# Second graph attention of a two-layer network: weighted sums of a head pair in two goes of 12 and 10 key tiles, earlier reciprocals, a bf16 mask

## What is computed

```python
qkv = x @ Wqkv + bqkv                                  # x: [2708, 256], 4 heads of 64
scores = einsum('hnd,hmd->hnm', qh, kh) * SCALE
scores = scores + graph_bias * adj_matrix
scores = where(attn_mask == 0, -1e9, scores)           # adj_matrix = attn_mask = adj
attn = softmax(scores, axis=-1)
out = einsum('hnm,hmd->hnd', attn, vh)
return out @ Wout + bout
```

## Time and profile before

| what | us |
|---|---|
| median of 3 runs (2942.5 to 2944.53) | 2943.89 |
| the profiled execution, own time | 2962.46 |
| its span, first to last instruction | 2960.5 |
| PE busy | 2559.8 (86%) |
| DVE busy | 2115.6 (71%) |
| ACT busy | 1793.5 (61%) |
| POOL busy | 1485.8 (50%) |

### The profile page before, as it was taken

The page is one execution under the profiler, slowest core; times in us unless marked ns, Lnnn a source line. Parts: engine busy times, 40 slices in busy tenths (PEclk is TensorE's granted clock), DMA queues, the critical chain, the costliest instruction groups (busy, mean ns, idle before and its releaser), DMA issues. The chain is left out here.

```text
span 2960.5 us, 62129 instructions
## 1 busy us (share of the span) xinstructions
PE 2559.8 (86%) x20638; PEld 2083.9 (70%) x20725; DVE 2115.6 (71%) x4364; ACT 1793.5 (61%) x3207; POOL 1485.8 (50%) x1752
## 2 busy tenths in 40 slices
PE   6698888888871599636899999999959999999999
PEld 5466666666661599416767777777748888888888
DVE  5799999999963244256587787787766777777776
ACT  1688888888840133114466666666646777777775
POOL 5755666665523311363122122122138888888886
PEclk9899999999985799757999999999989999999999
DMA  5011111111134222211011111111000000000001
GB/s 197 19 39 52 42 37 37 37 37 37 38 129 145 73 71 71 73 39 50 6 39 42 54 37 40 54 37 40 35 7 0 0 0 0 0 0 0 0 0 38
DMA packets 53520, 122.55 MB, mean 41 GB/s; under 512 B 7402, under 2 KB 38734, under 8 KB 47822
## 3 DMA queue, kind: packets, MB, share of 16 engines
q1 hardware_dynamic: 46350, 102.28, 10.0%
q0 software_dynamic: 7104, 19.41, 2.0%
HBM read 97.39 MB, written 24.27 MB: 41 GB/s over the span
## 5 line engine op out<-in xcount | busy, mean ns | idle before, releaser
L1974 PE MATMUL f_pm<-f_wl,f_yt 128*128 128x256 f32 x2640 | 625.7, 380 | 0.0
L1974 PEld LDWEIGHTS f_pm<-f_wl,f_yt 128*128 128x128 f32 x2640 | 477.2, 191 | 51.6
L515 POOL TENSOR_SCALAR a_off<-ADJ 128x677 bf16<-128x677 f32 x88 | 284.4, 3254 | 271.8 <-DMA ADJ<-in_adj 260.1
L1022 POOL TENSOR_TENSOR ADJ<-ADJ,a_off 128x2708 f32<-128x2708 f32 x22 | 131.3, 5969 | 537.4 <-DVE ADJ L1101 537.4
L116 POOL TENSOR_SCALAR f_yy<-f_th,f_rs 128x255 f32<-128x255 f32 x660 | 367.7, 575 | 21.8 <-POOL f_rs L111 21.8
L1824 DVE SCALAR_TENSOR_TENSOR f_gg<-f_th,f_pm 128x512 f32<-128x512 f32 x319 | 218.9, 686 | 167.8 <-ACT f_th L1918 166.7
L587 DVE SCALAR_TENSOR_TENSOR a_lg<-a_fo,F,a_low 128x1024 f32<-128x1024 f32 (+1 forms) x264 | 296.9, 1152 | 37.0 <-ACT a_low L536 23.5
L1918 ACT ACTIVATE f_th<-f_pm 128x512 f32<-128x512 f32 x319 | 190.6, 597 | 200.1 <-PE f_pm L1974 200.1
L1081 DVE CUSTOM_DVE_ANT_0 a_sc<-a_qk,ADJ 128x1024 f32<-128x1024 f32 (+1 forms) x264 | 288.1, 1092 | 30.7 <-PE a_qk L1179 30.7
L536 ACT ACTIVATE a_low<-a_fo,F2S 128x1024 f32<-128x1024 f32 (+1 forms) x264 | 259.0, 1018 | 78.7 <-PE a_fo L664 77.6
L1045 ACT ACTIVATE a_sc<-a_sc,a_mx 128x1024 f32<-128x1024 f32 (+1 forms) x264 | 277.7, 1052 | 42.3 <-DVE a_mx L1086 42.3
(11 more groups left out here) (256 smaller groups left out, 4986.9 us busy)
## 6 DMA issues: line engine op xcount, KB each, us to landing
ADJ<-in_adj SPq DMA_DIRECT2D x44, 1354.0 KB, 5.9
W<-in_L_ffn_w SPq DMA_DIRECT2D x32, 512.0 KB, 10.0
XD<-p_zeros SPq DMA_DIRECT2D x1, 7680.0 KB
m_rows<-XD SPq DMA_DIRECT2D x60, 128.0 KB, 2.0
YD<-m_y POOLq DMA_DIRECT2D x60, 128.0 KB, 2.0
out<-X SPq DMA_DIRECT2D x21, 128.0 KB
X<-in_x SPq DMA_DIRECT2D x3, 768.0 KB, 9.6
p_wqkv<-in_L_gnn_Wqkv SPq DMA_DIRECT2D x1, 768.0 KB, 4.4
```

Of the source, the lines that this page charges most:

```text
L515: pool.tensor_scalar(off[:, b, cols], adj[:, b, cols], 0.0, -HUGE, ALU.is_equal, ALU.mult).then_inc(off_done[b], 1)
L1974: mm = pe.matmul(out, yt[:, g, r, k, :], wl[:, k, :], start=(k == 0), stop=(k == KD - 1))
```

## The change

The weights of a pair get one buffer for all 22 key tiles. `weighted` runs twice per pair: tiles 0 to 11 (48 records of the trace) at the end of the pair's own chunk 2, tiles 12 to 21 (40 records) at the end of chunk 0 of the next pair. Chunk 1 has none. The reciprocals move on VectorE from chunk 1, behind `project`, to chunk 0, behind `heads`. The mask `off` becomes bf16 and its value -2^30.

```diff
-MASKED = -1e9
+MASKED = -2.0 ** 30
...
+HALF = 12
...
-        off = ph.sb("off", [P, N])
+        off = ph.sb("off", [P, N], BF16)
...
-        wt = ph.sb("wt", [P, 2, 2, CT, P])
+        wt = ph.sb("wt", [P, 2, NT, P])
...
-            copy(wt[:, (hp * NC + c) % 2, s, j - c * CT:end - c * CT, :],
+            copy(wt[:, s, j:end, :],
...
-                    if c == 0 and pair_before(i, b, hp):
-                        heads(*pair_before(i, b, hp))
+                    if c == 0:
+                        if pair_before(i, b, hp):
+                            heads(*pair_before(i, b, hp))
+                        reciprocals(i, b, hp)
                     if c == 1:
...
-                        reciprocals(i, b, hp)
...
-            def weighted(i, b, hp, c):
+            def weighted(i, b, hp, half):
 
-                if c == 0 and pair_before(i, b, hp):
+                if half == 0 and pair_before(i, b, hp):
                     pe.wait_ge(heads_out, pairs(*pair_before(i, b, hp)))
-                for g, (j0, end) in enumerate(chunk_groups(c)):
-                    for s in range(2):
-                        group = ("turn", hp, s, c, g)
-                        pe.wait_ge(copied[bank(group)], uses(i, b, group))
-                    for j in range(j0, end):
+                first, end = ((0, HALF), (HALF, NT))[half]
+                for c in range(NC):
+                    for g, (j0, j1) in enumerate(chunk_groups(c)):
+                        if max(first, j0) >= min(end, j1):
+                            continue
                         for s in range(2):
-                            mm = pe.matmul(po[s * HD:(s + 1) * HD, 0:P], V[:, j, 2 * hp + s, 0:HD],
-                                           wt[:, (hp * NC + c) % 2, s, j - c * CT, :],
-                                           start=(j == 0), stop=(j == NT - 1))
-                if c == NC - 1:
+                            group = ("turn", hp, s, c, g)
+                            pe.wait_ge(copied[bank(group)], uses(i, b, group))
+                        for j in range(max(first, j0), min(end, j1)):
+                            for s in range(2):
+                                mm = pe.matmul(po[s * HD:(s + 1) * HD, 0:P], V[:, j, 2 * hp + s, 0:HD],
+                                               wt[:, s, j, :], start=(j == 0), stop=(j == NT - 1))
+                if half:
                     mm.then_inc(heads_in, 1)
...
-                    if c:
-                        weighted(i, b, hp, c - 1)
-                    elif pair_before(i, b, hp):
-                        weighted(*pair_before(i, b, hp), NC - 1)
+                    if c == NC - 1:
+                        weighted(i, b, hp, 0)
+                    elif c == 0 and pair_before(i, b, hp):
+                        weighted(*pair_before(i, b, hp), 1)
...
-            weighted(NPAIR - 1, 1, HPAIR - 1, NC - 1)
+            weighted(NPAIR - 1, 1, HPAIR - 1, 1)
```

## The result

The changed kernel takes 3033.39 us, the median of six runs (3030.64 to 3039.96). The kernel before takes 2943.89 on the same chip, the median of five runs (2942.50 to 2945.22); a sixth run took 11528.47 us and is left out. The ratio is 1.0307, with a 95% interval of 1.0296 to 1.0318: 89.5 us slower. Forecast were 3053 us, and 3008 to 3096 as the range.

What follows compares the result with a forecast made beforehand. The second attention was taken as bound by VectorE's chain behind each anchor, then by TensorE's own work. Uncovered records 71.8, GpSimd 2.5 and clock falls 35 summed to +109 us on 2943.9: 3053 us, range 3008 to 3096.

Steps and rivals of the forecast that it cites:

- The chain behind the anchor: From TensorE's end of chunk 0's weighted sums, VectorE's work sets 7.86 or 6.13 us; freeing TensorE there gains 0.
- 32 records of 0.055 us, uncovered: Records moved to chunk 2 and next chunk 0, where TensorE never waits: 1.75 us in 41 pairs, +71.8 us.
- The clock: In the second attention, 41 new TensorE waits lower its granted clock, 1.7 us per fall: +35 us, between 0 and 70.
- I take half: Half of the 41 new TensorE waits are followed by a clock fall: 20.5 x 1.7 = +35 us.
- GpSimd: Mask addition with bf16 goes from 5969 ns to 8.4 us, hidden except once at the stage's start: +2.5 us.
- VectorE's bf16 write: Making the mask in bf16 stays at 1.56 us: 0; rival of halved rate +28 us, 3081, chance 0.04.
- the reciprocals: Moved on VectorE to chunk 0 behind `heads`: 0, at most 0.53 us per pair either way.
- The dropped go: One go of weighted sums fewer per pair on TensorE: 0.23 us beside its records, 0.3 taken as the most.
- the rival: TensorE alone bounds the second attention; a dropped go gives 0.3 us in 43 pairs: 13 us less, 2931, chance 0.06.

Runs made afterwards that it cites:

- e1: The changed kernel with the weighted sums back in the old three goes of 8, 8 and 6 tiles: 2944.92 us.
- e2: The changed kernel, with TensorE multiplying the first 8 tiles once more at the end of chunk 1, result thrown away: 3021.94 us.
- e5: The changed kernel with VectorE's mask and adjacency scaling moved from chunks 0 and 1 to the end of chunk 2 of pair hp = 1: 2965.79 us.
- e6: The changed kernel with VectorE taking project ahead of chunk 1's second score instead of behind it: 2992.57 us.
- e3: The changed kernel with the reciprocals back in chunk 1, behind project: 3036.57 us.
- e4: The kernel before with only the bf16 mask and its new value: 2941.33 us, ratio 0.9993.
- e9: The kernel before, three goes kept, with mask and scaling moved to chunk 2 and project ahead of chunk 1's second score: 2936.15 us.
- e8: The changed kernel with its go of 12 tiles at the end of chunk 1, 10 at the end of the next chunk 0: 2931.05 us.
- e10: e8 with goes of 8 tiles at the end of chunk 1 and 14 at the end of the next chunk 0: 2943.77 us.
- e11: e8 with VectorE's mask and scaling moved to the end of chunk 2 and project ahead of chunk 1's second score: 2975.03 us.
- e7: The changed kernel with VectorE's mask and scaling at the end of chunk 2 and project ahead of chunk 1's second score: 2932.06 us.
- e12: e11 with the reciprocals at the end of chunk 1: 2951.00 us.

## Why the prediction was right

**The chain behind the anchor, right.** Predicted were 7.86 and 6.13 us, unchanged; measured 7.91 and 6.07. Predicted were 20 waits ahead of `shares` and 21 ahead of chunk 2's turn, and about 1 us in the last block. There are 20 for `shares` and 21 for L1128, the last of them 1.21 us; the first block waits 2.07 us for the small copy that stands in `project`'s place there. e1 and e2 show from two sides that they, and not TensorE's work, set the stretch, and e5 and e6 that either is VectorE's own.

**32 records of 0.055 us, uncovered, right.** 41 x 1.75 = 71.8 us. The stage grew by 89.4, less 18.8 of clock: 70.6. Anchors were predicted 17.4 and 17.9 us apart; they are 17.79 for hp = 0, and 19.09 for hp = 1 with a fall of 1.7 in it, so 17.4. A block was to grow from 31.7 to 35.2 us, and one without a fall takes 35.18.

**The clock, right in kind, too large.** The step mis-sized was "I take half": 20.5 falls, 35 us. There were 11, 18.8 us. The price of one, 1.7 us, was right. What I missed is that the two kinds of waits differ: none of the 18 unbroken waits of 1.77 us for L1128 was followed by a fall, while 10 of the 20 for `shares`, 0.45 and 1.57 us close together, were, and so was the first of the two waits of 1.96 for L1128. That is 16 of the 20 us by which 3053 was too high. That `shares` came to exactly half is luck: e6 has the same 20 pairs of waits and 6 falls. And the waits that the guess was read from were pairs as well. Each of the nine in the earlier trace rows has one of 0.6 us behind it, and the two falls came with the second:

```profile
519.63 1.50 PE L677 MATMUL a_tp<-ident,a_lg 128*128 128x128 f32 x6 [0.62 <-DVE a_wt L492]
```

A wait of 1.56 us with one of 0.62 behind it is not an unbroken shorter one. The Trainium skill's advice on idle gaps ("TensorE: Matmul & The Clock Gate", why this matters for your kernels), by which there would be no fall, does not hold here: the clock fell behind 13 of e3's waits of 2.05 to 2.10 us, and the changed kernel lost 18.8 us to its 11 falls.

**GpSimd, wrong in sign.** +2.5 us was taken from L521's rate. The addition with a bf16 mask is not slower but faster:

```profile
L1023 POOL TENSOR_TENSOR ADJ<-ADJ,a_off x22: 5302/5335/5355, 1452.9 to 2187.4; 128x2708 f32<-128x2708 f32 x22
```

5335 ns for 5969. L521 works on pieces of a quarter, in another stage; its rate did not carry over, and no run tells why. The step matters 3 us.

**VectorE's bf16 write and the reciprocals, right.** L1097 has 1.57 us for 1.56, and e3 and e4 price both edits at nothing.

**The dropped go, too dear in the rival.** 0.3 us per go was read from TensorE's rows alone. e9 against e8 gives 0.10 at most, e10 none: where the go stood, other small gaps open.

## What to carry to other kernels

A short wait on the busiest engine can be the visible end of a long one that other work covers. Before work is moved away from in front of it, walk the other engine's chain from the last point where the two meet, and see which is longer. Goes may be merged, if the merged one stands where the cover was: the same two goes were 3% slower or 0.4% faster. And moving the other engine's work pays only as long as it is not late at the next meeting point.

## What was not expected of the hardware

- A small VectorE copy from SBUF to SBUF (L1112, 128x128 f32) was held until the end of GpSimd's addition of two SBUF tensors, 60 times of 60 that it met one: 1.62 us instead of 0.23 in e11, 0.76 to 0.95 in e5 and e7, ending 0.08 to 0.09 us behind the addition. It took 0.23 again when moved (e12, 24 us faster). A reciprocal of 2 columns just ahead of it, during the same addition, took its usual 0.17 us, and a score of 1024 columns its 1.22. The Trainium skill ("GPSIMD Engine Reference", specifications) names contention on the SBUF interfaces that the two engines share, for VectorE's two-port mode or two SBUF inputs. The copy has one SBUF input, so by that it would be the two-port mode; the runs show the hold and its price, and not the mode.
- More work made TensorE's stage shorter: 88 us of repeated matmuls in the waits (e2) saved 11, by keeping the clock at 2.4 GHz.
- Waits of 1.77 us left the clock up 54 times of 54 (the changed kernel, e3 and e5, 18 each). Of the six waits of 1.96 us in these kernels three were followed by a fall, of the 20 of 2.05 to 2.10 us in e3 13. The pair of 0.45 and 1.57 us was followed by one 10 times of 20 in the changed kernel and 6 of 20 in e6. So the length of a wait alone does not decide it; what else does, no run here tells.
